# Rotary query product of a cross-attention kernel: weights stored twice side by side, nine matmuls instead of six, no doubling copy

## Chip, cores and metric

The kernel runs on one core of a Trainium2 chip. The metric is the device time of one execution in microseconds (us), the median of three runs. Engines are called PE (matmuls), DVE (vector), ACT (scalar), POOL (GpSimd) and SP (whose queue issues DMAs).

## What is computed

One block of cross-attention with multi-head latent projections, then a feed-forward block with ternary weights; batch 2, 512 query tokens of width 512, 1024 context rows of width 128, 16 heads.

```python
q_hk = (hidden_q @ Wq.T).reshape(B, S, H, K)                   # S = 512, H = 16, K = 128
q_big = _apply_rope(einsum('bshk,hkq->bshq', q_hk, w_kc_q))    # 384 wide
kv_r = _apply_rope(kv_c, sin_k, cos_k)
q_r = einsum('bshq,hqr->bhsr', q_big, W_qr)                    # R = 64: the product that is changed
k_r = einsum('bld,hdr->bhlr', kv_r, W_kr)
attn = softmax(einsum('bhsr,bhlr->bhsl', q_r, k_r))
ctx_c = einsum('bhsl,bld->bhsd', attn, kv_r)
ctx_lat = einsum('bhsd,hkd->bhsk', ctx_c, w_kc_kv)
x = x + ctx @ Wo.T
x = x + ffn(layernorm(x))      # ternary weights, activations rounded to 8 bits
```

## The kernel before

All is kept transposed, features on partitions, 512 tokens of one batch b in the free dimension. Each float32 operand of a matmul is split into a high part (rounded to float32r) and a low part (the rest), and a product is the sum of three matmuls: high by high, high by low, low by high (`three`). The work of a head is cut into groups, each of which fills one of four PSUM banks (`banks`):

- A(b): query projection, 12 matmuls; B(b, c), c = 0 to 2: its 384-wide expansion, 3 matmuls each. DVE (and for some ACT and POOL) multiplies B by cosines and sines into `rot_cos` and `rot_sin`; POOL adds them (L1055), rounds to `rot_hi` (L1061) and takes the rest `rot_lo` (L1063).
- C(b): the rotary query product with `W_qr`, 64 wide, over three chunks c. This is the group that is changed.
- K(b, half): keys; score(u), u = 0 to 7: four matmuls for 128 tokens by 1024 keys into `scores`; DVE "max" (L1323), ACT "exp" (L1185), ACT "high" (L1196) and DVE "low" (L1330) make the fp16 softmax rows; SP "turn" transposes them by DMA (L943) into `pt`.
- V(b): rows by values, 24 matmuls in 8 parts; M: the product of the two output weights; O(b, j): output, added to `acc` by DVE (L1318).

A(b), B and C of the next head are made during this one. A program for each engine runs through tables: `EVEN_PE`, `ODD_PE`, `EVEN_ACT` and so on list what the engine does in an even or odd head, in that order; `OPEN_*` is the first head with all its preparation, `LAST_*` the sixteenth. Heads 1 to 14 run as seven pairs of an odd and an even head with the same order. Engines wait on each other by semaphores: `group_full` counts groups that PE has finished, `group_hi` those whose high part ACT has taken out, `group_read` those that DVE has emptied, in DVE's order. SP loads the weights of later heads into one buffer, `load`, one lot after another (WQ, WC, WRK, WVO), each when POOL has split the one before (L386, L388).

C(b) before. The 128 columns of `wr` hold the high half of a 64-wide weight and its low half side by side. Two matmuls a chunk (`rot_hi`, then `rot_lo`, L1461) leave the high weight's product on partitions 0 to 63 and the low weight's on 64 to 127. The scores need the query on both halves, since a key tile has its high part on one half and its low part on the other. So ACT copies partitions 0 to 63 twice into `qr_hi` (L1143, L1159); DVE subtracts `qr_hi` from them into `rest` (L1270), waits for itself, and adds partitions 64 to 127 into the upper half of `qr_lo` (L1273); and ACT, some items later, copies that half to the lower one ("double", L1177). A score waits for `doubled`.

In the table of an even head ACT has "M, exp 4, high 4, C(0), exp 5, high 5, B(1, 2), double 0, V(0)"; DVE has "max 4, M, B(1, 0), B(1, 1), max 5, C(0), low 4, low 5, B(1, 2), V(0)"; PE has "score 4, M, C(0) parts 0 and 1, B(1, 0), C(0) part 2, B(1, 1), score 5, V(0)...". C(1) comes last in all three: PE begins it after O(0, 3) (even) or O(0, 0) (odd), and its part 2 is the last thing before the next head.

Of the kernel before, what the change touches and what calls it, by code (L numbers as in the profile page):

```python
# [74 lines left out]
UNGROUPED = ("score", "max", "exp", "sum", "double", "abs", "drop", "stats", "spread", "root", "deviation", "norm", "extreme", "scale", "X", "take", "first root",  # L75
# [27 lines left out]
    ("B", 0, 2, "next"), V1, ("exp", 2), ("high", 2), ("exp", 3), ("double", 1, "last"), ("high", 3), A1, ("abs", 2),  # L103
    ("M",), ("exp", 4), ("high", 4), C0, ("exp", 5), ("high", 5), ("B", 1, 2, "next"), ("double", 0, "next"), V0,
# [4 lines left out]
    ("high", 2), ("exp", 3), ("high", 3), ("double", 1, "last"), A1, ("M",), ("abs", 0), ("exp", 4), C0, ("high", 4),  # L109
    ("exp", 5), ("high", 5), ("K", 0, 0, "next"), ("K", 0, 1, "next"), ("B", 1, 2, "next"), V0, ("double", 0, "next"),  # L110
# [61 lines left out]
    ("double", 1, "last"), ("exp", 3), ("high", 3), ("exp", 4), ("high", 4), ("drop", 1), ("exp", 5), ("high", 5),  # L172
# [496 lines left out]
class SecondNorm:  # L669


    def __init__(self, nc, ctx, t):
# [115 lines left out]
def attention_heads(nc, ins, pack, sources, biases, out, t, early, raw, second):  # L788
# [3 lines left out]
    with ExitStack() as ctx:  # L792
# [339 lines left out]
        def scalar_heads(act):  # L1132
            def high_part(p, marked):
# [68 lines left out]
            def period(p):  # L1202
                for item in p.act:
# [871 lines left out]
```

## Time and profile before

| | |
|---|---|
| median of 3 runs | 858.98 us (858.0 to 860.82) |
| profiled execution, span from first to last instruction | 861.5 us |
| PE, DVE, ACT, POOL busy | 88%, 89%, 67%, 67% |
| PE clock granted | 0.97 on average, 1.00 between 84 and 667 us |
| one pair of heads | 83.3 us, seven times |
| head 0 with its preparation; last head and feed-forward | about 84 us; 194.5 us |

The profile gives the span of its execution, and no other time of it. The span is 2.5 us above the median of the runs. A busy PE is not PE at its peak: one matmul of 512 columns is shown as 0.39 us, but in a dense stretch the next begins 0.23 us later, so that their spans overlap. A DVE operation likewise overlaps the next by some 0.08 us.

### The profile page before, as it was taken

What the parts mean: (1) busy time and instruction counts of PE and PEld (TensorE: products, weight loads), DVE (VectorE), ACT (ScalarE), POOL (GpSimd) and SP (SyncE); (2) the same over time, 40 slices, a digit from 0 to 9 for tenths busy, and PEclk for the clock granted to TensorE, in tenths of its full rate; (3) what the DMA queues carried; (4) which work ended last, traced back from release to release, by engine and by line L of the source; (5) the groups of instructions that cost most, each with busy time, mean ns of one, the idle gap of its engine ahead of it and who ended that gap; (6) DMA issues with size and microseconds to landing.
All of it is one profiled execution on the core that took longest, in us unless ns stands there. A gap on an engine that the chain in (4) does not pass through costs nothing.

```text
span 861.5 us, 12578 instructions
## 1 busy us (share of the span) xinstructions
PE 757.3 (88%) x3268; PEld 487.1 (57%) x3268; DVE 766.2 (89%) x1026; ACT 573.6 (67%) x838; POOL 577.6 (67%) x581
## 2 busy tenths in 40 slices
PE   3678998989999999999999999999999675868996
PEld 3555565756666666666566656665666442424543
DVE  5799899989998999899989999999999767797895
ACT  2477677767766867687667766776777576774332
POOL 5769674867486757766776668576848474867462
PEclk9889999999999999999999999999999797889999
DMA  9216867776768576858676766677668999400000
GB/s 330 79 49 115 169 130 140 138 167 134 151 114 170 117 161 132 170 111 167 118 160 134 152 128 138 149 137 150 125 146 213 241 227 275 164 0 25 13 24 37
DMA packets 294405, 118.50 MB, mean 138 GB/s; under 512 B 271856, under 2 KB 278000, under 8 KB 294128
## 3 DMA queue, kind: packets, MB, share of 16 engines
q1 hardware_dynamic: 293568, 116.68, 62.0%
q10 hardware_dynamic: 816, 1.57, 0.5%
q8 instruction: 9, 0.15, 0.1%
q14 instruction: 12, 0.10, 0.0%
HBM read 49.02 MB, written 2.10 MB: 59 GB/s over the span
## 4 chain that ended last, share of the span: by engine, by line
PE 35%; POOL 20%; DVE 18%; issue 11%; DMA 7%; SPq 5%; ACT 3%; POOLq 1%; DVEq 0%; ACTq 0%
PE banks L1419 22%; POOL rot_cos L1055 5%; PE scores L1720 5%; DMA load<-in_pack 4%; POOL rot_lo L1063 4%; SPq L943 4%; PE scores L1507 3%; PE banks L1735 3%; DVE neg_max L1323 3%; POOL rot_hi L1061 2%; DVE rows L1330 2%; POOL rot_sin L1046 2%; DVE rot_cos L1295 2%; DVE cv_lo L1288 1%; POOL wq_lo L388 1%
## 5 line engine op out<-in xcount | busy, mean ns | idle before, releaser
L1185 ACT ACTIVATE scores<-scores,neg_max 128x1024 f32<-128x1024 f32 x128 | 139.2, 1087 | 56.1 <-DVE neg_max L1323 54.6
L1330 DVE SCALAR_TENSOR_TENSOR rows<-scores,rows 128x1024 f16<-128x1024 f32 x128 | 154.9, 1220 | 13.7 <-ACT rows L1196 12.6
L1419 PE MATMUL banks<-pt,v_hi 128*128 128x512 f16 x512 | 154.3, 383 | 12.5 <-DMA pt<-rows 11.4
L1323 DVE TENSOR_REDUCE neg_max<-scores 128x1 f32<-128x1024 f32 x128 | 155.5, 1216 | 2.9 <-PE scores L1507 2.7
L1055 POOL TENSOR_TENSOR rot_cos<-rot_cos,rot_sin 128x512 f32<-128x512 f32 x93 | 119.2, 1281 | 46.6 <-DVE rot_sin L1297 42.2
L1196 ACT ACTIVATE rows<-scores 128x1024 f16<-128x1024 f32 x128 | 130.8, 1022 | 5.2
L1063 POOL TENSOR_TENSOR rot_lo<-rot_cos,rot_hi 128x512 fp32r<-128x512 f32 x93 | 119.6, 1286 | 7.8
L1159 ACT CAST cv_hi<-banks 128x512 fp32r<-128x512 f32 x64 | 37.6, 587 | 102.6 <-PE banks L1419 101.4
L1318 DVE SCALAR_TENSOR_TENSOR acc<-banks,inv,acc 128x512 f32<-128x512 f32 x128 | 91.4, 745 | 8.0 <-PE banks L1419 4.1
L1419 PE MATMUL banks<-pt,v_lo 128*128 128x512 f16 x256 | 97.8, 382 | 0.0
L1419 PEld LDWEIGHTS banks<-pt,v_hi 128*128 128x128 f16 x512 | 44.5, 98 | 79.2 <-issue 36.4
L1946 POOL TENSOR_TENSOR hidden<-sigma,val 128x512 f32<-128x512 f32 x32 | 46.0, 1439 | 35.5 <-DVE val L1788 26.4
L1288 DVE TENSOR_TENSOR cv_lo<-banks,cv_hi 128x512 fp32r<-128x512 f32 x64 | 44.1, 689 | 26.2 <-ACT cv_hi L1159 25.1
L1061 POOL TENSOR_SCALAR rot_hi<-rot_cos 128x512 fp32r<-128x512 f32 x93 | 57.6, 619 | 14.3 <-POOL rot_cos L1055 13.3
L1720 PE MATMUL scores<-ternary,xt 128*128 128x512 bf16 x256 | 62.2, 394 | 5.3 <-DVE gate L1788 3.3
L1419 PE MATMUL banks<-m_hi,cv_hi 128*128 128x512 f32 x128 | 53.4, 417 | 14.4 <-DVE cv_lo L1288 14.4
L1419 PE MATMUL banks<-x_hi,wq_hi 128*128 128x512 f32 x128 | 53.1, 415 | 10.7 <-DVE x_lo L634 6.4
L1507 PE MATMUL scores<-kr_odd,qr_hi 128*128 128x512 f32 x128 | 57.2, 447 | 5.4 <-DVE rows L1330 5.4
L1507 PE MATMUL scores<-kr_even,qr_hi 128*128 128x512 f32 x128 | 55.0, 429 | 2.0 <-issue 2.0
L1419 PE MATMUL banks<-cv_hi,wc_hi 128*128 128x512 f32 x96 | 42.3, 441 | 12.9 <-POOL wc_lo L388 5.5
L1419 PE MATMUL banks<-x_lo,wq_hi 128*128 128x512 f32 x128 | 52.0, 406 | 0.0
L1419 PE MATMUL banks<-x_hi,wq_lo 128*128 128x512 f32 x128 | 51.9, 405 | 0.0
(211 smaller groups left out, 1824.7 us busy)
## 6 DMA issues: line engine op xcount, KB each, us to landing
load<-in_pack SPq DMA_DIRECT2D x15, 320.0 KB, 3.5
raw_chunk<-in_out_w SPq DMA_DIRECT2D x8, 512.0 KB, 5.2
raw_chunk<-in_gate_w SPq DMA_DIRECT2D x8, 512.0 KB, 4.4
raw_chunk<-in_val_w SPq DMA_DIRECT2D x8, 512.0 KB, 4.6
raw<-in_gate_w SPq DMA_DIRECT2D x8, 512.0 KB, 5.5
raw<-in_val_w SPq DMA_DIRECT2D x8, 512.0 KB, 5.2
raw<-in_out_w SPq DMA_DIRECT2D x8, 512.0 KB, 7.0
load<-in_pack SPq DMA_DIRECT2D x15, 256.0 KB, 3.3
```

Source lines behind the costliest of these rows:

```text
L1055: nc.gpsimd.tensor_tensor(total, total, rot_sin[:, c, :], ALU.add).then_inc(rot_sum, 1)
L1061: nc.gpsimd.tensor_scalar(hi, total, 1.0, 0.0, ALU.mult, ALU.add).then_inc(rot_hi, 1)
L1063: nc.gpsimd.tensor_tensor(lo, total, hi.bitcast(F32), ALU.subtract).then_inc(rot_ready, 1)
L1185: nc.scalar.activation(scores[:, u % 2, :], scores[:, u % 2, :], ACT.Exp, bias=neg_max[:, u:u + 1], accum_out=sums[:, u:u + 1]).then_inc(e ...
L1196: nc.scalar.activation(rows[:, u % ROWS, 0, :], scores[:, u % 2, :], ACT.Copy, scale=WEIGHT_LIFT).then_inc(weights_hi, 1)
L1288: return nc.vector.tensor_tensor(pair[1], src, pair[0].bitcast(F32), ALU.subtract)
L1318: return nc.vector.scalar_tensor_tensor(out=t["acc"][:, u, :], in0=src, scalar=inv[:, u:u + 1], in1=t["acc"][:, u, :], op0=ALU.mult, op1=A ...
L1323: nc.vector.tensor_reduce(neg_max[:, u:u + 1], scores[:, u % 2, :], AX, ALU.max, negate=True).then_inc(max_ready, 1)
L1330: nc.vector.scalar_tensor_tensor(out=rows[:, u % ROWS, 1, :], in0=scores[:, u % 2, :], scalar=WEIGHT_LIFT, in1=rows[:, u % ROWS, 0, :], op ...
L1419: mm = nc.tensor.matmul(out, ws[a], xs[c], start=first and n == 0, stop=last and n == 2)
L1507: mm = nc.tensor.matmul(scores[:, u % 2, half * 512:(half + 1) * 512], qr[low][:, b, j * P:(j + 1) * P], kr[odd][:, b, half * 512:(half + ...
L1720: mm = nc.tensor.matmul(ps_gv[:, n % 4, :], x, w[:, c, part_of(n // 2)], start=c == 0, stop=c == KD - 1)
```

## The change

- `wr` becomes `wr_hi` and `wr_lo`, each 128 columns: the 64 columns of a chunk twice side by side. POOL splits 128x384 elements instead of 128x192, from a source read twice.
- C takes three matmuls a chunk, nine in all instead of six, through `three` (the product of the two low parts, which the doubled arrangement had, is not made). Both halves of the partitions hold the whole query.
- ACT takes `qr_hi` out in one copy of 128x512, DVE `qr_lo` in one subtraction of 128x512. `rest`, its semaphore, the "double" items and `doubled` go; a score waits on `group_read` for C(b).
- The buffers of the second normalization's statistics move over `wv` to make room.

```diff
     def rotated(h, src):
-        split(h, 2, [t["wr"][:, :, half, :] for half in range(2)],
-              src[:, 0:CQ * R].rearrange("p (c r) -> p c r", c=CQ)).then_inc(wr_ready, 1)
+        split(h, 2, [w[:] for w in t["wr"]],
+              src[:, 0:CQ * R].rearrange("p (c o r) -> p c o r", c=CQ, o=1).broadcast_to([P, CQ, 2, R])).then_inc(wr_ready, 1)
...
                 elif kind == "C":
-                    src = banks[0:R, p.bank[marked], :]
-                    nc.scalar.copy(qr[0][0:R, group[1], :], src)
-                    out = qr[0][R:2 * R, group[1], :]
+                    out = qr[0][:, group[1], :]
...
-            def double(p, marked):
-
-                b = marked[1]
-                done = p.earlier(("C", b, "next")) if marked[-1] == "last" else p.place(("C", *marked[1:]))
-                act.wait_ge(group_read, p.read(done))
-                nc.scalar.copy(qr[1][0:R, b, :], qr[1][R:2 * R, b, :]).then_inc(doubled, 1)
-
...
-                    if kind == "C":
-
-
-                        b, low = group[1], slice(R, 2 * R)
-                        nc.vector.tensor_tensor(rest[low, b, :], banks[0:R, bank, :], qr[0][0:R, b, :].bitcast(F32),
-                                                ALU.subtract).then_inc(rest_ready, 1)
-                        dve.wait_ge(rest_ready, h.after(B, b + 1))
-                        return nc.vector.tensor_tensor(qr[1][low, b, :], banks[low, bank, :], rest[low, b, :], ALU.add)
...
                     if kind == "A":
                         pair = [x[:] for x in q]
+                    elif kind == "C":
+                        pair = [x[:, group[1], :] for x in qr]
...
-                        for half in range(2):
-                            mm = nc.tensor.matmul(out, wr[:, c].rearrange("p o r -> p (o r)"), rot[half][:, c, :],
-                                                  start=c + half == 0, stop=c + half == CQ)
+                        mm = three(out, [w[:, c].rearrange("p o r -> p (o r)") for w in wr], [x[:, c, :] for x in rot],
+                                   c == 0, c == CQ - 1)
...
                 odd = p.head.number % 2
+                places = [p.place(("C", b)) if p.first else p.earlier(("C", b, "next"))]
                 if not odd:
                     here = b or p.first
-                    pe.wait_ge(group_read, p.read(*(p.place(("K", b, half)) if here else p.earlier(("K", 0, half, "next"))
-                                                    for half in range(2))))
-                pe.wait_ge(doubled, p.head.after(B, b + 1))
+                    places += [p.place(("K", b, half)) if here else p.earlier(("K", 0, half, "next")) for half in range(2)]
+                pe.wait_ge(group_read, p.read(*places))
```

DVE in an even head, at C(0) of the next head, from max 5 to low 4 and low 5; before:

```order
L1323 TENSOR_REDUCE neg_max<-scores 128x1 [waits scores_full]
L1262 REGISTER_ALU
L1270 TENSOR_TENSOR rest<-banks,qr_hi 64x512 [waits group_hi]
L1272 REGISTER_ALU
L1273 TENSOR_TENSOR qr_lo<-banks,rest 64x512 [waits rest_ready]
L1330 SCALAR_TENSOR_TENSOR rows<-scores,rows 128x1024 [waits weights_hi] x2
```

and with the change:

```order
L1305 TENSOR_REDUCE neg_max<-scores 128x1 [waits scores_full]
L1250 REGISTER_ALU
L1270 TENSOR_TENSOR qr_lo<-banks,qr_hi 128x512 [waits group_hi]
L1312 SCALAR_TENSOR_TENSOR rows<-scores,rows 128x1024 [waits weights_hi] x2
```

Two operations with a wait between them have become one; what is before and behind them stays.

ACT at the same place, from exp 5 of the even head to V(0); before:

```order
L1143 CAST qr_hi<-banks 64x512 [waits group_full]
L1159 CAST qr_hi<-banks 64x512
L1184 REGISTER_ALU
L1185 ACTIVATE scores,sums<-scores,neg_max 128x1024 [waits max_ready]
L1196 ACTIVATE rows<-scores 128x1024 [waits row_turned1,exp_ready]
L1136 REGISTER_ALU
L1165 REGISTER_ALU [waits group_full]
L1169 COPY rot_sin<-banks 64x512 [waits rot_ready]
L1170 COPY rot_sin<-banks 64x512
L1176 REGISTER_ALU
L1177 COPY qr_lo<-qr_lo 64x512 [waits group_read]
```

and with the change:

```order
L1156 CAST qr_hi<-banks 128x512 [waits group_full]
L1174 REGISTER_ALU
L1175 ACTIVATE scores,sums<-scores,neg_max 128x1024 [waits max_ready]
L1186 ACTIVATE rows<-scores 128x1024 [waits row_turned1,exp_ready]
L1135 REGISTER_ALU
L1162 REGISTER_ALU [waits group_full]
L1166 COPY rot_sin<-banks 64x512 [waits rot_ready]
L1167 COPY rot_sin<-banks 64x512
```

The second copy of `qr_hi` and the doubling copy are gone, and exp 5 and high 5 keep their places.

## Rows read from the trace of the kernel before

**Rows 1.** The page: share of busy time, and the chain that ended last by engine.

```profile
PE 757.3 (88%) x3268; PEld 487.1 (57%) x3268; DVE 766.2 (89%) x1026; ACT 573.6 (67%) x838; POOL 577.6 (67%) x581
...
PE 35%; POOL 20%; DVE 18%; issue 11%; DMA 7%; SPq 5%; ACT 3%; POOLq 1%; DVEq 0%; ACTq 0%
```

**Rows 2.** Windows, heads 1 to 14: stretch, length, busy (instructions) by engine, PE clock.

```profile
84.00:667.00 583.00, 548.61 (x2340) 367.67 (x2339) 547.20 (x687) 419.51 (x645) 405.33 (x434) 1.00 0.71 145
```

**Rows 3.** Groups by line and form: busy us, mean ns | idle before it.

```profile
L1159 ACT CAST cv_hi<-banks 128x512 fp32r<-128x512 f32 x64 | 37.6, 587 | 102.6 <-PE banks L1419 101.4
L388 POOL TENSOR_TENSOR wr<-load,wr 128x192 fp32r<-128x192 f32 x15 | 8.9, 591 | 1.2
L386 POOL TENSOR_SCALAR wr<-load 128x192 fp32r<-128x192 f32 x15 | 5.3, 351 | 52.0 <-DMA load<-in_pack 52.0
L388 POOL TENSOR_TENSOR wc_lo<-load,wc_hi 128x384 fp32r<-128x384 f32 x15 | 16.0, 1070 | 1.2
L386 POOL TENSOR_SCALAR wc_hi<-load 128x384 fp32r<-128x384 f32 x15 | 7.7, 513 | 43.2 <-DMA load<-in_pack 43.2
```

**Rows 4.** Timeline of PE, even head: start, length, operation. C(0) part 0; B(1, 0).

```profile
490.87 0.39 PE L1461 MATMUL banks<-rot_hi,wr 128*128 128x512 f32 x1
...
491.77 0.40 PE L1419 MATMUL banks<-cv_hi,wc_hi 128*128 128x512 f32 x1
...
492.24 0.40 PE L1419 MATMUL banks<-cv_hi,wc_lo 128*128 128x512 f32 x1
```

**Rows 5.** Timeline of DVE, same place: M, B(1, 0), max 5, C(0), low 4.

```profile
491.86 0.75 DVE L1282 SCALAR_TENSOR_TENSOR m_lo<-banks,m_unit,m_hi 128x512 fp32r<-128x512 f32 x1
492.67 0.69 DVE L1295 TENSOR_TENSOR rot_cos<-banks,cos 128x512 f32<-128x512 f32 x1
...
495.08 1.22 DVE L1323 TENSOR_REDUCE neg_max<-scores 128x1 f32<-128x1024 f32 x1
496.32 0.69 DVE L1270 TENSOR_TENSOR rest<-banks,qr_hi 64x512 f32<-64x512 f32 x1
...
497.77 2.36 DVE L1330 SCALAR_TENSOR_TENSOR rows<-scores,rows 128x1024 f16<-128x1024 f32 x2
```

**Rows 6.** Timeline of POOL, then PE: from the even head to A(0) in the odd one.

```profile
495.24 1.27 POOL L1055 TENSOR_TENSOR rot_cos<-rot_cos,rot_sin 128x512 f32<-128x512 f32 x1 [0.58 <-DVE rot_sin L1297]
507.06 0.62 POOL L386 TENSOR_SCALAR wq_hi<-load 128x512 fp32r<-128x512 f32 x1 [0.21 <-DMA load<-in_pack]
506.90 0.50 PE L1461 MATMUL banks<-rot_hi,wr 128*128 128x512 f32 x1 [0.63 <-POOL rot_lo L1063]
509.11 0.50 PE L1419 MATMUL banks<-x_hi,wq_hi 128*128 128x512 f32 x1 [0.46 <-POOL wq_lo L388]
```

**Rows 7.** Timeline, second half of an odd head: ACT exp 5, high 5; DVE; POOL; PE.

```profile
453.19 1.09 ACT L1185 ACTIVATE scores<-scores,neg_max 128x1024 f32<-128x1024 f32 x1 [0.33 <-DVE neg_max L1323]
454.42 1.02 ACT L1196 ACTIVATE rows<-scores 128x1024 f16<-128x1024 f32 x1
454.63 2.36 DVE L1330 SCALAR_TENSOR_TENSOR rows<-scores,rows 128x1024 f16<-128x1024 f32 x2
460.63 1.29 POOL L1046 TENSOR_TENSOR rot_sin<-rot_sin,sin 128x512 f32<-128x512 f32 x1 [1.75 <-DVE rot_cos L1265]
465.58 0.51 PE L1461 MATMUL banks<-rot_hi,wr 128*128 128x512 f32 x1 [0.30 <-POOL rot_lo L1063]
```

**Rows 8.** Timeline: PE in head 0; DVE at the end of head 14.

```profile
57.66 0.79 PE L1419 MATMUL banks<-cv_hi,wc_hi 128*128 128x512 f32 x1 [3.05 <-DVE qr_lo L1273]
...
675.33 0.68 DVE L1270 TENSOR_TENSOR rest<-banks,qr_hi 64x512 f32<-64x512 f32 x1
676.78 1.23 DVE L1323 TENSOR_REDUCE neg_max<-scores 128x1 f32<-128x1024 f32 x1
```

**Rows 9.** Timeline of POOL, odd head: first rotation behind the key split; its wait for M.

```profile
518.77 1.29 POOL L1055 TENSOR_TENSOR rot_cos<-rot_cos,rot_sin 128x512 f32<-128x512 f32 x1
531.43 0.30 POOL L386 TENSOR_SCALAR wv_hi<-load 128x128 fp32r<-128x128 f32 x1 [0.98 <-PE banks L1419]
```

More of the change, by code:

```diff
@@ L74 @@
 A0, A1, V1, V0, C0, C1 = ("A", 0, "next"), ("A", 1, "next"), ("V", 1, "last"), ("V", 0), ("C", 0, "next"), ("C", 1, "next")
-UNGROUPED = ("score", "max", "exp", "sum", "double", "abs", "drop", "stats", "spread", "root", "deviation", "norm", "extreme", "scale", "X", "take", "first root",
+UNGROUPED = ("score", "max", "exp", "sum", "abs", "drop", "stats", "spread", "root", "deviation", "norm", "extreme", "scale", "X", "take", "first root",
              "turn", "start root", "values", "count", "variance", "inverse", "normed", "rotate", "products", "rotated",
@@ L102 @@
     ("high", 7, "last"), ("K", 1, 0), A0, ("K", 1, 1), ("exp", 0), ("high", 0), ("exp", 1), ("high", 1),
-    ("B", 0, 2, "next"), V1, ("exp", 2), ("high", 2), ("exp", 3), ("double", 1, "last"), ("high", 3), A1, ("abs", 2),
-    ("M",), ("exp", 4), ("high", 4), C0, ("exp", 5), ("high", 5), ("B", 1, 2, "next"), ("double", 0, "next"), V0,
+    ("B", 0, 2, "next"), V1, ("exp", 2), ("high", 2), ("exp", 3), ("high", 3), A1, ("abs", 2),
+    ("M",), ("exp", 4), ("high", 4), C0, ("exp", 5), ("high", 5), ("B", 1, 2, "next"), V0,
     ("exp", 6), ("high", 6), ("exp", 7), C1,
@@ L108 @@
     ("high", 7, "last"), A0, ("exp", 0), ("high", 0), ("exp", 1), ("high", 1), ("B", 0, 2, "next"), V1, ("exp", 2),
-    ("high", 2), ("exp", 3), ("high", 3), ("double", 1, "last"), A1, ("M",), ("abs", 0), ("exp", 4), C0, ("high", 4),
-    ("exp", 5), ("high", 5), ("K", 0, 0, "next"), ("K", 0, 1, "next"), ("B", 1, 2, "next"), V0, ("double", 0, "next"),
+    ("high", 2), ("exp", 3), ("high", 3), A1, ("M",), ("abs", 0), ("exp", 4), C0, ("high", 4),
+    ("exp", 5), ("high", 5), ("K", 0, 0, "next"), ("K", 0, 1, "next"), ("B", 1, 2, "next"), V0,
     ("exp", 6), ("high", 6), ("abs", 1), ("exp", 7), C1,
@@ L143 @@
     ("turn", "x", 4), ("turn", "x", 5), ("turn", "k", 1), ("abs", 2), ("rotate", 0, 0), ("rotate", 0, 1),
-    ("rotate", 0, 2), ("A", 1), ("abs", 0), ("C", 0), ("turn", "k", 0), ("double", 0), ("abs", 1), ("spread most",),
-    A0, ("K", 0, 0), ("K", 0, 1), ("Y", 3), ("values", 0), ("values", 1), ("C", 1), ("exp", 0), ("double", 1),
+    ("rotate", 0, 2), ("A", 1), ("abs", 0), ("C", 0), ("turn", "k", 0), ("abs", 1), ("spread most",),
+    A0, ("K", 0, 0), ("K", 0, 1), ("Y", 3), ("values", 0), ("values", 1), ("C", 1), ("exp", 0),
     ("high", 0), ("exp", 1), ("high", 1), ("Y", 2), ("K", 1, 1), ("M",), ("B", 0, 2, "next"), ("exp", 2), ("high", 2),
     ("K", 1, 0), ("exp", 3), ("high", 3), A1, ("exp", 4), ("high", 4), C0, ("exp", 5), ("high", 5),
-    ("B", 1, 2, "next"), ("double", 0, "next"), V0, ("exp", 6), ("high", 6), ("exp", 7), C1,
+    ("B", 1, 2, "next"), V0, ("exp", 6), ("high", 6), ("exp", 7), C1,
 )
@@ L171 @@
     ("high", 7, "last"), ("exp", 0), ("high", 0), ("exp", 1), ("high", 1), ("exp", 2), ("drop", 0), ("high", 2), V1,
-    ("double", 1, "last"), ("exp", 3), ("high", 3), ("exp", 4), ("high", 4), ("drop", 1), ("exp", 5), ("high", 5),
+    ("exp", 3), ("high", 3), ("exp", 4), ("high", 4), ("drop", 1), ("exp", 5), ("high", 5),
     ("drop", 2), ("exp", 6), ("drop", 3), ("M",), ("high", 6), V0, ("exp", 7), ("first root",), ("high", 7),
@@ L684, in __init__, with at @@
         self.links = 0
-    def at(self, rows):
+    def at(self, rows, place):
         self.rows = rows
+        self.stats = self.nc.alloc_sbuf_tensor_at("stats_second", [P, NU, 6], F32, offset=place)
+        self.mv = self.nc.alloc_sbuf_tensor_at("mv_second", [P, NU, 2], F32, offset=place + 24 * NU)
     def tile(self, u):
@@ L804, in attention_heads @@
         qr = [placed(f"qr_{x}", [P, B, S], F32R) for x in ("hi", "lo")]
-        rest = nc.alloc_sbuf_tensor_at("rest", [P, B, S], F32, offset=at["qr_lo"])
         kr = [placed(f"kr_{x}", [P, B, L], F32R) for x in ("even", "odd")]
@@ L828, in attention_heads @@
         raw.open(nc.sbuf_base, at)
-        second.at(nc.alloc_sbuf_tensor_at("normed_rows", [P, U, D], F32, offset=at["kr_even"]))
+        second.at(nc.alloc_sbuf_tensor_at("normed_rows", [P, U, D], F32, offset=at["kr_even"]), at["wv"])
         loaded, split_hi = t["loaded"], t["split_hi"]
         wq_ready, wc_ready, wr_ready, wk_ready, wv_ready, wo_ready = t["ready"]
-        rest_ready, doubled = sem("rest_ready"), sem("doubled")
         rot_sum, rot_hi, rot_ready = sem("rot_sum"), sem("rot_hi"), sem("rot_ready")
@@ L1209, in period @@
                         start.spread_most(act)
-                    elif item[0] == "double":
-                        double(p, item)
                     elif item[0] == "abs":
@@ L2008, in xattn_ffn @@
                 stack = early if side == "right" else heads
+                t["places"][name] = (nc.sbuf_base + 31) // 32 * 32
                 t[name] = [stack.enter_context(nc.sbuf_tensor(f"{name}_{half}", shape, F32R, side=side))
                            for half in ("hi", "lo")]
-            t["wr"] = early.enter_context(nc.sbuf_tensor("wr", [P, CQ, 2, R], F32R, side="right"))
+            t["wr"] = [early.enter_context(nc.sbuf_tensor(f"wr_{half}", [P, CQ, 2, R], F32R, side="right")) for half in ("hi", "lo")]
             for name in ("loaded", "split_hi", "pair_loaded", "pair_hi"):
```

1 line of the change is left out of this document (removed).

## The prediction

> **What bounds the kernel now.** I read the page first. PE is busy 88% of the span and DVE 89%, ACT and POOL 67%; the chain that ended last passes through PE for 35%, POOL 20%, DVE 18% [rows 1]. So no engine is the bound by itself: a ring of waits through several engines is. The windows say where. Heads 1 to 14 take 583 of 861.5 us, all at full PE clock, 83.3 us a pair of heads [rows 2]. The pair is therefore what has to be costed, times seven. In it I went to the timelines of the engines and noted, at each place near a C group, who waits for whom. In a dense stretch PE starts a matmul of 512 columns each 0.225 to 0.235 us: C(0) parts 0 and 1 are four matmuls between 490.87 and 491.77, and two of B(1, 0) lie between 491.77 and 492.24 [rows 4].
>
> **What the change takes away.** On DVE a C group now fills 496.32 to 497.77, 1.45 us, two operations of 0.69 and a wait [rows 5]. The subtraction that replaces them is a two-operand operation of 128x512 out of PSUM, like the four of B(1, 0) and B(1, 1), which take 492.67 to 495.08, 0.60 each with what overlaps [rows 5]. The relief is 0.84 us a group, four groups a pair: 3.4 us. On ACT two copies of 64x512 become one, which takes 0.587 as `cv_hi` does [rows 3], and the doubling copy goes. ACT relief: about 1.2 us a group, but ACT is the idlest on the ring. It counts only where DVE waits for `qr_hi`.
>
> **What it adds.** Three matmuls a C group, 0.23 each: 2.8 us a pair on PE. On POOL the split of `wr` goes from 0.351 + 0.591 to what `wc`, of the same 128x384, takes: 0.513 + 1.070, so 0.64 us a head [rows 3]. That the source is read twice has no row; the floor is no growth, the ceiling twice the old 0.94, and I take `wc`'s, since the number of elements written is the same. A score's wait on `group_read` instead of `doubled` costs nothing: C(0) is emptied by 497.77 [rows 5] and first used after 506.90 [rows 6], and C(1) is emptied before the fourth score of its head begins.
>
> **One pair, followed by its delays.** I start where part 2 of C(1) ends an odd head: PE has waited 0.30 us for `rot_lo` at 465.58 [rows 7]. Its third matmul: **+0.23**. PE is dense from there to the end of A(0). DVE waits for A(0) (its earlier relief at C(1) is spent in that wait), so all of the even head so far is late by 0.23. M, then C(0) parts 0 and 1: two more matmuls, +0.47. B(1, 0) follows them on PE, ends at 492.24 + 0.40, and DVE takes it out at 492.67, 0.03 us later, having just come to the end of M (491.86 + 0.75) [rows 4, 5]. So DVE is late by 0.70, and behind part 2 (+0.23, of which some 0.06 was DVE's own queue) by **0.87** from B(1, 1) on. The relief of C(0) on DVE comes only behind that, at 496.32. But the ring leaves DVE before it: POOL's rotation of B(1, 0) waits for `rot_sin` of B(1, 1) (idle 0.58 before 495.24) and POOL then runs without a gap to 506.8, to `wq_hi` at 507.06, before which it had 0.21 idle for a load; A(0) of the odd head waits for `wq_lo` [rows 6]. Of the 0.21 I take 0.13 as slack (my estimate; POOL needs the rest to issue): A(0) is late by **0.74**. C(1) of the even head is hidden: its parts 0 and 1 lie in PE's wait for `rot_lo` (0.63 idle before part 2, 506.90), its part 2 in the wait for `wq_lo` (0.46 idle before 509.11) [rows 6].
>
> Odd head: late by 0.74 at A(0), hence at V(1) and O, hence PE is dense to C(0). B(1, 0) is again taken out by a waiting DVE: 0.74 + 0.47; B(1, 1) and max 5: 0.74 + 0.70 - 0.06 = **1.38**. Here DVE's relief is inside the ring, because POOL next waits for DVE's B(1, 2) (idle 1.75 before 460.63) [rows 7], which stands behind C(0), low 4 and low 5. Low 4 would start 0.84 earlier than the delay says. Low 5 cannot: it needs high 5 on ACT, high 5 needs exp 5, and exp 5 waited for max 5 (0.33 idle), late by 1.38. Before, high 5 ended at 454.42 + 1.02 = 455.44 and low 5 began at 454.63 + 2.36 - 1.22 = 455.77 [rows 7], so of the 0.84 only this 0.33, less 0.04 for a semaphore, comes through: 1.38 - 0.29 = **1.09** at low 5, at B(1, 2), at POOL, and at part 2 of C(1), which waits for this POOL chain (0.30 idle before 465.58). Parts 0 and 1 are again in its wait. POOL's 0.64 for `wr` falls behind a DMA and, in the odd head, makes the first rotation (518.77, no idle before it) late by 1.3; it ends in the 0.98 that POOL waits for M before 531.43 [rows 9]. If that cover were gone, it would add up to 0.6 a pair.
>
> So a pair grows by **1.09 us**, 83.3 to 84.4, seven pairs: +7.6.
>
> **The ends.** In head 0 PE is far from dense and DVE bounds: B(0, 0) of head 1 waits 3.05 us for the bank that `qr_lo` of C(1) holds [rows 8]. Two C groups stand in DVE's dense queue before it: -1.7. C(0) of head 1, made there too, stands before a wait for transposed rows. At the end of head 14, C(1) leads straight into max 0 of the last head: ACT copies `qr_hi`, DVE works on it from 675.33, max 0 begins at 676.78 [rows 8]. One copy less (0.58) and 0.84 less on DVE, until score 0 itself is the bound: -1.1. Sum: 7.6 - 1.7 - 1.1 = +4.8. Profiled span: 861.5 to 866.3; from the median of 858.98: **863.8 us**.
>
> At the matmul price the Trainium skill differs (TensorE: Matmul & The Clock Gate, Back-to-back issue gap): it states some 131 ns per matmul of 512 columns in a sustained stream. The trace disagrees, 225 ns and more [rows 4]. By the page's figure, the seven matmuls a pair that I put on the ring would cost 0.7 us less, the pair would grow by about 0.4, and the sum would come out at no change, 859.
>
> **Rivals.**
> (A) The relief wins. DVE has the highest share [rows 1], and if the PE delay at B(1, 0) is swallowed (were DVE itself late there by as much as PE), the relief of both C(0) of a pair passes on: 7 x 2 x 0.84 = 11.8, and the ends 2.8: 844. For it: DVE ends M only 0.06 us before it takes B(1, 0) [rows 5], so it is all but late itself. Against it: all but is not enough, since the two matmuls bring 0.46. It decides if DVE comes to B(1, 0) more than 0.5 us after PE.
> The Trainium skill (Perfetto Trace Analysis, Identifying the Most-Contended Engine) tells one to relieve the engine of highest occupancy first; by that rule this is the outcome. The trace is against it so far: occupancies of 88 and 89% are alike, and the chain has twice as much of PE as of DVE.
> (B) They cancel. If the whole 0.84 in the odd head comes through (exp 5 not being what holds low 5), a pair grows by 1.38 - 0.84 = 0.54, and 3.8 - 2.8 leaves +1.0: 860. For it: ACT and DVE are only 0.3 us apart there. Against it: ACT cannot start exp 5 before max 5.
> (C) PE is the bound. All 84 added matmuls of heads 1 to 14 add up: 84 x 0.23 = 19.3, less 2.8 at the ends: +16.5, 875.5. For it: between 84 and 667 us PE is busy 548.6 of 583 [rows 2]. Against it: those spans overlap, and it waits 0.30 and 0.63 us for `rot_lo` just behind parts 0 and 1 of C(1) and 0.46 for `wq_lo` [rows 6, 7]. It decides once those waits are used up. POOL's split without its cover would be half way, 868.
>
> **How the numbers follow.** Forecast 0.52 (862 to 868), B 0.2, A 0.15, C 0.13. The range takes in B and C and leaves out A at its full price, 0.15: below, 852, half of A's gain, since how far DVE's relief gets is what I am least sure of; above, 876. A measurement of this kernel can tell some 0.3%, 2.6 us, from no change. Slower: the forecast but for its lower edge, and C, 0.58; within 0.3%: most of B and that edge, 0.2; faster: A, and what of B falls below, 0.22.
>
> **What would show it.** Right: the pair at 84.2 to 84.6 us; DVE idle about 0.7 us before B(1, 0) in both heads; low 5 of the odd head waiting for `rows` of ACT; POOL's waits at rotations of B(1, 0) and B(1, 2) as now or longer; C on PE 0.68 us a part; `qr_lo` 0.69. DVE busy some 22 us less over the span, with more idle. Wrong: a pair of 83.3 or less (A or B), with DVE going into B(1, 0) without idle; or of 86 (C), with no wait of PE left for `rot_lo`. If the wait for `wv_hi` on POOL is gone, the split was uncovered.

## The result and the profile after

| | before | with the change |
|---|---|---|
| median time | 860.09 us (856.54 to 866.47, 20 runs) | 865.25 us (860.19 to 870.69, 20 runs) |
| ratio, 95% interval | 1 | 1.0056 (1.0038 to 1.0074) |
| profiled execution, span | 861.5 us | 860.4 us |
| a pair of heads, in the trace | 83.31 us | 84.38 us |
| PE, DVE, ACT, POOL busy | 88, 89, 67, 67% | 90, 86, 62, 68% |

The change is slower by 0.56%, 5.2 us between the medians. The two profiled spans say the opposite, 861.5 and 860.4 us. They are one execution each. Their difference comes from one place: behind the M of the last head the execution of before takes 150.6 us and that of the change 143.2. Over the other twelve profiles of this study this stretch lies between 143.4 and 147.2 us, and the medians of the times don't follow it. So the spans can't be compared to a few microseconds. The heads can: in one execution the same distance comes back within 0.1 us in most pairs. The mark for a head is the start of ACT's `m_hi`, once a head. In the timeline of ACT, heads 10, 11 and 12 with the change:

```profile
495.13 0.69 ACT L1147 ACTIVATE m_hi<-banks,m_unit 128x512 fp32r<-128x512 f32 x1
...
535.79 0.69 ACT L1147 ACTIVATE m_hi<-banks,m_unit 128x512 fp32r<-128x512 f32 x1 [1.00 <-PE banks L1401]
...
579.52 0.69 ACT L1147 ACTIVATE m_hi<-banks,m_unit 128x512 fp32r<-128x512 f32 x1
```

Before, these marks are at 491.15, 531.23 and 574.48. Over the marks of heads 3 to 14 the median pair grows by 1.07, from 83.31 to 84.38. From the M of head 0 to that of head 14, seven pairs, it adds up to 7.65 us (the first pair grows by 0.63, the second by 1.64, the other five by 0.99 to 1.13). The M of head 0 comes 1.49 us earlier (64.87 to 63.38), and the last stretch, M of head 14 to M of the last, grows by 0.13. Together the last M is late by 6.3 us; the interval of the ratio holds 3.3 to 6.4.

Where a pair is cut into halves, the mark is the start of PE's last matmul of M. `m_hi` starts 0.42 or 0.43 us behind it in nearly all these heads. In the even heads of the kernel before it is 0.51, since ACT comes there from another item. That would move 0.08 us from one half to the other; the pair is the same to 0.01 by either mark. Timeline of PE and of ACT, head 10, before:

```profile
490.64 0.39 PE L1419 MATMUL banks<-wo_hi,wv_lo 128*128 128x512 f32 x1
```

```profile
491.06 0.19 ACT L1252 ACTIVATION_READ_ACCUMULATOR raw_chunk<-raw_chunk  x1
491.15 0.67 ACT L1150 ACTIVATE m_hi<-banks,m_unit 128x512 fp32r<-128x512 f32 x1
```

By PE's mark the way from the even M to the odd one was 40.14 us and is 40.65; from the odd to the even it was 43.16 and is 43.72.

The page of the change, busy time and chain, to be held beside [rows 1], and the window of heads 1 to 14 beside [rows 2]:

```profile
PE 771.4 (90%) x3364; PEld 504.5 (59%) x3364; DVE 741.3 (86%) x994; ACT 532.9 (62%) x774; POOL 588.2 (68%) x581
...
PE 31%; POOL 27%; issue 13%; DVE 12%; DMA 7%; SPq 5%; ACT 3%; POOLq 1%; DVEq 0%; ACTq 0%
```

```profile
84.00:667.00 583.00, 556.98 (x2388) 380.38 (x2387) 520.54 (x651) 379.33 (x582) 408.11 (x429) 1.00 0.70 142
```

DVE has lost 25 us of work and 6 points of the chain, and the kernel is slower. That is the lesson of the case: 25 us came off the engine with the highest share, and the time grew, because some of the added matmuls (14 us of busy time on PE) lie in front of what DVE waits for.

The groups that answer to [rows 3], by line:

```profile
L1270 DVE TENSOR_TENSOR qr_lo<-banks,qr_hi 128x512 fp32r<-128x512 f32 x32 | 21.8, 681 | 0.0
L388 POOL TENSOR_TENSOR wr_lo<-load,wr_hi 128x384 fp32r<-128x384 f32 x15 | 15.0, 1001 | 1.3
```

With its source read twice the subtraction for `wr` takes 1.00 us, about what that for `wc` takes (1.07), as the prediction had it. Now the place of [rows 4, 5] in the even head. Timeline of PE, the third matmul of C(0) part 0 and the first of B(1, 0):

```profile
495.39 0.39 PE L1401 MATMUL banks<-rot_hi,wr_lo 128*128 128x512 f32 x1
...
496.30 0.40 PE L1401 MATMUL banks<-cv_hi,wc_hi 128*128 128x512 f32 x1
```

Timeline of DVE: M, B(1, 0), max 5, C(0) in one operation, low 4, low 5:

```profile
495.91 0.74 DVE L1264 SCALAR_TENSOR_TENSOR m_lo<-banks,m_unit,m_hi 128x512 fp32r<-128x512 f32 x1
497.20 0.69 DVE L1277 TENSOR_TENSOR rot_cos<-banks,cos 128x512 f32<-128x512 f32 x1 [0.55 <-PE banks L1401]
...
499.80 1.22 DVE L1305 TENSOR_REDUCE neg_max<-scores 128x1 f32<-128x1024 f32 x1
500.93 0.68 DVE L1270 TENSOR_TENSOR qr_lo<-banks,qr_hi 128x512 fp32r<-128x512 f32 x1
501.53 1.22 DVE L1312 SCALAR_TENSOR_TENSOR rows<-scores,rows 128x1024 f16<-128x1024 f32 x1
503.34 1.22 DVE L1312 SCALAR_TENSOR_TENSOR rows<-scores,rows 128x1024 f16<-128x1024 f32 x1 [0.60 <-ACT rows L1186]
```

DVE has an idle of 0.55 before B(1, 0) that it did not have, and what it saved at C(0) ends in the 0.60 before low 5. Timeline of POOL from there, for [rows 6]:

```profile
499.96 1.27 POOL L1054 TENSOR_TENSOR rot_cos<-rot_cos,rot_sin 128x512 f32<-128x512 f32 x1 [1.22 <-DVE rot_sin L1279]
...
511.58 0.62 POOL L386 TENSOR_SCALAR wq_hi<-load 128x512 fp32r<-128x512 f32 x1
```

The rotation waits 1.22 instead of 0.58, and the 0.21 for a load that POOL had before `wq_hi` is gone.

### The profile page after: what moved, and what is told of

The parts are those of the page before. It is cut to its first block, busy times and chain, and to the rows that moved or that the text cites. A ratio compares the mean times of both kernels' runs of the same rounds, so it can differ in the third digit from the quotient of the medians.

```text
span 860.4 us, 12617 instructions
## 1 busy us (share of the span) xinstructions
PE 771.4 (90%) x3364; PEld 504.5 (59%) x3364; DVE 741.3 (86%) x994; ACT 532.9 (62%) x774; POOL 588.2 (68%) x581
## 4 chain that ended last, share of the span: by engine, by line
PE 31%; POOL 27%; issue 13%; DVE 12%; DMA 7%; SPq 5%; ACT 3%; POOLq 1%; DVEq 0%; ACTq 0%
PE banks L1401 20%; POOL rot_cos L1054 7%; PE scores L1701 4%; DMA load<-in_pack 4%; POOL rot_lo L1062 4%; SPq L942 3%; POOL rot_hi L1060 3%; PE scores L1488 3%; POOL rot_sin L1045 2%; PE banks L1716 2%; DVE neg_max L1305 2%; POOL wq_lo L388 2%; POOL wo_lo L388 2%; DVE rows L1312 1%; DMA pt<-rows 1%
```

## The experiments

All ran in five rounds beside the kernel before, and each ratio is to the runs of before on the same chip. The pair is the median over heads 3 to 14 of the profiled execution. "Even" is the distance on PE from the even M to the odd one, "odd" from the odd to the even.

| run | even | odd | pair | ratio, 95% interval |
|---|---|---|---|---|
| before | 40.14 | 43.16 | 83.31 | 1 |
| the change | 40.65 | 43.72 | 84.38 | 1.0056 (1.0038 to 1.0074) |
| six matmuls | 39.94 | 42.84 | 82.79 | 0.9936 (0.9912 to 0.9960) |
| before, nine matmuls | 41.05 | 43.98 | 85.04 | 1.0101 (1.0076 to 1.0125) |
| narrow split | 40.65 | 43.73 | 84.36 | 1.0047 (1.0025 to 1.0069) |
| six in C(1) only | 40.66 | 43.50 | 84.15 | 1.0040 (1.0012 to 1.0069) |
| DVE in pieces | 41.30 | 44.29 | 85.59 | 1.018 (1.0149 to 1.021) |
| ACT in halves | 40.69 | 43.71 | 84.43 | 1.0066 (1.0041 to 1.0090) |
| one part ahead | 40.68 | 43.47 | 84.14 | 1.0026 (1.0003 to 1.0049) |
| one part ahead, load ahead | 41.34 | 43.47 | 84.76 | 1.0079 (1.0048 to 1.0110) |
| load ahead alone | 42.06 | 43.74 | 85.78 | 1.0151 (1.0110 to 1.0192) |
| six, one part and load ahead | 41.12 | 42.69 | 83.78 | 1.0002 (0.9981 to 1.0023) |
| six, one part ahead | 39.98 | 42.66 | 82.64 | 0.9919 (0.9886 to 0.9952) |
| before, one part ahead | 39.99 | 42.95 | 82.94 | 0.9960 (0.9935 to 0.9986) |

### The two halves of the change, apart

Six matmuls: all of the change but the third matmul.

```diff
-                        mm = three(out, [w[:, c].rearrange("p o r -> p (o r)") for w in wr], [x[:, c, :] for x in rot],
-                                   c == 0, c == CQ - 1)
+                        for half in range(2):
+                            mm = nc.tensor.matmul(out, wr[0][:, c].rearrange("p o r -> p (o r)"), rot[half][:, c, :],
+                                                  start=c + half == 0, stop=c + half == CQ)
```

> The changed kernel without its third matmul a chunk (the low part of the weight times the high part of the query is left out of the product), so PE does as many matmuls as before. My theory (a ring of waits: PE's matmuls before B(1, 0) and B(1, 1) are on it, DVE's relief at C(0) comes through only in the odd head and only by 0.29 us, since exp 5 and high 5 on ACT hold low 5): a pair of heads at 83.0 us, 0.3 under the kernel before, and with 2.8 us less at the ends a ratio to before of about 0.994. Rival A (DVE is the bound, all its relief comes through): a pair at 79.9, ratio about 0.97. Rival C (PE's count of matmuls is what counts): a pair at 83.3.

Nine matmuls on the kernel before: one matmul more a chunk and nothing else.

```diff
-                        for half in range(2):
+                        for n, half in enumerate((0, 1, 0)):
                             mm = nc.tensor.matmul(out, wr[:, c].rearrange("p o r -> p (o r)"), rot[half][:, c, :],
-                                                  start=c + half == 0, stop=c + half == CQ)
+                                                  start=c + n == 0, stop=c + n == CQ + 1)
```

> The kernel before with one more matmul a chunk in C (the first of the two is issued again and added once more, so the query product differs) and all else as it was: the cost on PE alone, with no relief on DVE or ACT. My theory: the even head late by 0.74, the odd by 0.64, a pair at 84.7 us, ratio to before about 1.012. PE the bound: 12 x 0.23 = 2.8 a pair, 86.1, ratio 1.022. DVE the bound: 83.3 to 83.5, ratio 1.00.

The signs are as expected and the sizes are larger. The matmuls cost a pair 85.04 - 83.31 = 1.73 us (or, from six to nine on the changed kernel, 84.38 - 82.79 = 1.59), where the prediction had 1.38. The relief gives 0.66 us (85.04 - 84.38) or 0.52 (83.31 - 82.79), where it had 0.29. Both prices miss by about as much and in opposite directions, so the sum came out.

Where the relief comes through is seen by halves. In the odd half it is 43.98 - 43.72 = 0.26, close to the 0.29 that low 5 lets through. The rest, 41.05 - 40.65 = 0.40, is in the even half, where the prediction had none. Its place is the V(1) that PE does next, at the start of the odd head. It needs the even head's rows 7 turned by SP, the turn waits for low 7, and low 7 stands behind C(1) on DVE. Timeline of PE, last matmul of B(0, 2) and first two of V(1): before, with the change, and with nine matmuls on the kernel before:

```profile
515.70 0.40 PE L1419 MATMUL banks<-cv_hi,wc_lo 128*128 128x512 f32 x1
516.10 0.59 PE L1419 MATMUL banks<-pt,v_hi 128*128 128x512 f16 x2
```

```profile
520.41 0.40 PE L1401 MATMUL banks<-cv_hi,wc_lo 128*128 128x512 f32 x1
520.65 0.60 PE L1401 MATMUL banks<-pt,v_hi 128*128 128x512 f16 x2
```

```profile
524.25 0.39 PE L1419 MATMUL banks<-cv_hi,wc_lo 128*128 128x512 f32 x1
524.86 0.59 PE L1419 MATMUL banks<-pt,v_hi 128*128 128x512 f16 x2 [0.22 <-DMA pt<-rows]
```

A dense matmul starts 0.23 us behind the one before it. V(1) starts 0.36, 0.24 and 0.61 behind (medians of five even heads). So it waited 0.13 for its rows before, doesn't with the change, and waits 0.38 with nine matmuls and no relief, which is all but 0.02 of the 0.40. Timeline of DVE in that last run at C(1) and low 7, and of SP at the turn of rows 7:

```profile
517.68 0.68 DVE L1270 TENSOR_TENSOR rest<-banks,qr_hi 64x512 f32<-64x512 f32 x1 [0.41 <-ACT qr_hi L1159]
...
519.12 1.23 DVE L1330 SCALAR_TENSOR_TENSOR rows<-scores,rows 128x1024 f16<-128x1024 f32 x1
```

```profile
520.43 1.84 SPq L943 DMA_TRANSPOSE pt<-rows  x1
```

DVE itself waits 0.41 there for ACT's second copy of `qr_hi`. So that copy and DVE's second operation both lie on the way to low 7.

### DVE's relief, ACT's relief and POOL's split

DVE in pieces: the changed kernel, its subtraction cut into four.

```diff
+                        for rows, cols in ((slice(0, 64), slice(0, 512)), (slice(64, 128), slice(0, 320)),
+                                           (slice(64, 96), slice(320, 512))):
+                            nc.vector.tensor_tensor(pair[1][rows, cols], src[rows, cols], pair[0][rows, cols].bitcast(F32),
+                                                    ALU.subtract)
+                        src, pair = src[96:128, 320:512], [x[96:128, 320:512] for x in pair]
```

> The changed kernel with DVE's subtraction of each C group done in four pieces, (rows 0 to 63, 512 columns), (64 to 127, 320), (64 to 95, 192), (96 to 127, 192), which by 0.60 us for 512 columns should fill about 1.5 us, as the two operations and the wait did before (1.45). So DVE's relief is taken back and all else of the change left. By the steps of the prediction only 0.29 us of it comes through in a pair: 84.37 to 84.7. By the run with nine matmuls on the kernel before (85.04) the relief of DVE and ACT together is worth 0.67: if it is all DVE's, 85.0.

Timeline of DVE, C(0) in pieces and low 4, low 5; then max 0 and A(0) of the odd head:

```profile
508.77 1.45 DVE L1265 TENSOR_TENSOR qr_lo<-banks,qr_hi 64x512 fp32r<-64x512 f32 x3
510.23 0.36 DVE L1275 TENSOR_TENSOR qr_lo<-banks,qr_hi 32x192 fp32r<-32x192 f32 x1
510.63 2.36 DVE L1317 SCALAR_TENSOR_TENSOR rows<-scores,rows 128x1024 f16<-128x1024 f32 x2
...
524.50 1.22 DVE L1310 TENSOR_REDUCE neg_max<-scores 128x1 f32<-128x1024 f32 x1
525.79 0.69 DVE L1275 TENSOR_TENSOR cv_lo<-banks,cv_hi 128x512 fp32r<-128x512 f32 x1
```

The pieces take 1.86 us (508.77 to 510.63), 0.36 more than meant, so the pair is above either figure, 85.59. The run doesn't measure the relief, but it shows that DVE's part of it matters in both halves. With 1.26 us put on DVE a group, the even half grows by 0.65 and the odd one by 0.57. Low 5 has lost its wait of 0.60. A(0) of the odd head has lost the 0.78 us for which DVE waited with the change (517.35, for ACT's `cv_hi`), and is 0.59 later behind M (22.22 us with the change, 525.79 - 502.98 = 22.81 here). V(1) waits for rows 7 again (0.57 behind the matmul before it, median), and `wq_hi` waits 0.61 for its load, which stands on SP behind the turns of rows 4 and 5 and so behind low 4.

ACT in halves: two copies of 64 rows for `qr_hi`.

```diff
+                    nc.scalar.copy(qr[0][0:64, group[1], :], src[0:64, :])
+                    out, src = qr[0][64:128, group[1], :], src[64:128, :]
```

> The changed kernel with ACT's copy of each C group done in two halves of 64 rows, as before the change (0.58 us each). By the prediction ACT's relief counts only where DVE waits for qr_hi, so nothing: pair 84.3 to 84.4 us. If the difference of 0.67 us a pair between nine matmuls on the kernel before and the changed kernel is partly ACT's, 84.6 or more.

84.43: 0.05 us, next to nothing. That doesn't show that ACT has no share in the relief. Low 7 starts 0.71 us later behind M here (514.97 - 494.76 against 514.21 - 494.71), and V(1) 0.28 instead of 0.24 behind the matmul before it (head 10): the copy has just used up V(1)'s cover, and whatever DVE adds to it counts. From nine matmuls on the kernel before (41.05) to this run (40.69) the even half loses 0.36 with ACT's second copy still in place, and the copy then gives 0.04. How much of the 0.40 would be ACT's in the other order, its copy gone and DVE's two operations left, no run shows. The doubling copy of `qr_lo` was not put back in any run.

Narrow split: from the third head on, POOL splits 128x192 elements and leaves the second copy of the weights as it was, so the lower half of the product is computed with older weights.

```diff
+        wide = h.i is None and h.number < 2
+        if wide:
...
+            return
+        split(h, 2, [w[:, :, 0, :] for w in t["wr"]],
+              src[:, 0:CQ * R].rearrange("p (c r) -> p c r", c=CQ)).then_inc(wr_ready, 1)
```

> The changed kernel, but from the third head on POOL splits only the first of the two copies of the weight, 128x192 elements as before; the second copy keeps an older head's values. It takes 0.64 us a head off POOL. My theory (the split is covered by POOL's wait for M and for sines): a pair as in the changed kernel, 84.4 us. If the split stood in the open: 83.7 (odd head) or 83.1 (both).

84.36 against 84.38: the 0.64 us a head on POOL is hidden. Little of it even reaches its cover in the odd head: POOL's wait before `wv_hi` is 0.99 here and 0.85 with the whole split.

### Which matmuls count

Six in C(1) only: the first diff above, for C(1) alone.

> The changed kernel with the third matmul (low half of the weights times high half of the rotated query) left out in C(1) only; C(0) keeps nine. By the steps of the prediction C(1) costs the pair only the third matmul of part 2 in the odd head, 0.23 us, all else of it being hidden in waits for rot_lo and wq_lo: pair 84.37 less 0.23, 84.1 to 84.2 us, with PE's wait for rot_lo before part 2 of the odd head at 0.5 to 0.6 us again. If PE is the bound, all six count: 84.37 less 1.4, 83.0.

Timeline of PE, odd head, part 2 of C(1):

```profile
551.59 0.50 PE L1447 MATMUL banks<-rot_hi,wr_hi 128*128 128x512 f32 x1 [0.38 <-POOL rot_lo L1062]
```

84.15, and all of the 0.23 comes out of the odd half. So of the six third matmuls in the C(1) groups of a pair one counts, as the prediction said, and C(0) is where the price is paid. The wait for `rot_lo` comes back at 0.38, not at 0.5 to 0.6, without a bearing on the pair. With the whole change it was all but gone: the timeline of PE at the same place, one pair earlier, has

```profile
469.12 0.40 PE L1401 MATMUL banks<-m_hi,cv_lo 128*128 128x512 f32 x1
469.44 0.50 PE L1401 MATMUL banks<-rot_hi,wr_hi 128*128 128x512 f32 x1
```

which is 0.32 us from start to start, 0.09 above a dense distance. So the two third matmuls of parts 0 and 1 are hidden by a narrow margin.

### Taking C(0) out of the way

In the changed kernel part 1 of C(0) goes behind B(1, 0) and part 2 behind B(1, 1), so that DVE gets B(1, 0) three matmuls sooner. The tables of even and odd heads change alike; the lines are shortened here.

```diff
-    ("M",), part(0, 3, C0), part(1, 3, C0), ("B", 1, 0, "next"), part(2, 3, C0), ("B", 1, 1, "next"), ("score", 5),
+    ("M",), part(0, 3, C0), ("B", 1, 0, "next"), part(1, 3, C0), ("B", 1, 1, "next"), part(2, 3, C0), ("score", 5),
```

> The changed kernel with PE's order M, C(0) part 0, B(1, 0), part 1, B(1, 1), part 2, where it was M, parts 0 and 1, B(1, 0), part 2, B(1, 1): one part, 0.69 us, less before each of the two. My theory: B(1, 1) late by 0.2 instead of 0.87, a pair at 83.2 to 83.5 us, ratio to before about 0.997. If the number of matmuls, not their place, costs the time: 84.4 as in the changed kernel, ratio 1.006.

84.14, where about 83.3 was expected. The first step went as expected. Behind M, the wait of 0.55 before B(1, 0) is gone, POOL starts its rotation 0.69 us earlier (498.91 - 494.77 = 4.14 us behind M, against 499.96 - 495.13 = 4.83), and `wq_hi` is split 0.68 earlier. Then it is lost again at two waits that were not in the reckoning. Timeline of SP, POOL and PE in the even half:

```profile
511.16 1.95 SPq L940 DMA_TRANSPOSE pt<-rows  x1
513.43 0.69 SPq L905 DMA_DIRECT2D load<-in_pack  x1
```

```profile
516.56 0.51 POOL L384 TENSOR_SCALAR wc_hi<-load 128x384 fp32r<-128x384 f32 x1 [4.02 <-DMA load<-in_pack]
```

```profile
518.30 0.47 PE L1399 MATMUL banks<-cv_hi,wc_hi 128*128 128x512 f32 x1 [1.79 <-POOL wc_lo L386]
```

The load of `wc` leaves SP 18.66 us behind M, as in the changed kernel (513.82 - 495.13 = 18.69), where `wq_lo` held it too. Now `wq_lo` is early, but SP's turn of rows 6 stands ahead of the load and waits for low 6, whose scores lie behind all nine matmuls of C(0) on PE. PE then waits 1.79 instead of 0.88 for `wc_lo`. In the odd half it is score 5, which stays behind the nine matmuls whatever their order, and which max 5, exp 5 and low 5 need. Timeline of DVE, max 5 of the odd head:

```profile
540.00 1.22 DVE L1303 TENSOR_REDUCE neg_max<-scores 128x1 f32<-128x1024 f32 x1 [0.34 <-PE scores L1486]
```

The next two runs put the load of `wc` ahead of that turn on SP, in even heads.

```diff
-    ("turn", 4), ("turn", 5), ("lot", 0), ("turn", 6), ("lot", 1),
+    ("turn", 4), ("turn", 5), ("lot", 0), ("lot", 1), ("turn", 6),
```

> The order with one part of C(0) ahead of B(1, 0), and on SP, in even heads, the load of wc placed before the turn of rows 6 instead of behind it. Theory W (a second wait next in line): with one part ahead, wq_lo of the odd head was split 0.68 us earlier behind M, yet the load of wc left SP at 18.66 us behind M as before, since SP's turn of rows 6 (16.39 to 18.34) stood ahead of it, and PE then idled 1.79 instead of 0.88 us for wc_lo. So this kernel should let the load go at about 18.0 us, the odd M come 40.1 to 40.3 us behind the even M (40.83 without it), and the pair fall from 84.1 to 83.5 us (83.3 to 83.7). Theory P (PE is dense and its added matmuls are simply the bound): no change, pair 84.1.

> The changed kernel with only the SP edit (in even heads the load of wc placed before the turn of rows 6), the order of PE as in the change. Theory W: the load waits for wq_lo too, which ends 18.44 us behind M, against 18.33 for the turn; so next to nothing, pair 84.3 to 84.4 us, and only the two edits together pay. Rival: the turn alone was the wait, pair 83.7.

The first half of the expectation holds: with both edits `wc_hi` is split at 517.01 - 496.13 = 20.88 us behind M instead of 21.79, and PE waits 0.89 for `wc_lo` instead of 1.79. But the pair gets longer, 84.76 where 83.5 was expected, and with the SP edit alone 85.78 where 84.3 to 84.4 was. Timeline of SP and PE with both:

```profile
508.28 6.13 SPq L905 DMA_DIRECT2D load<-in_pack  x2
514.58 5.30 SPq L940 DMA_TRANSPOSE pt<-rows  x2
```

```profile
522.56 0.59 PE L1399 MATMUL banks<-pt,v_hi 128*128 128x512 f16 x2 [1.48 <-DMA pt<-rows]
```

A load that waits holds the whole queue: the turns of rows 6 and 7 start at 514.58, one behind the other, and V(1) waits 1.48 us for them. The expectation named what was ahead of the load and not what would stand behind it.

Then the two orders with six matmuls, and PE's order on the kernel before.

> Six matmuls in C (low half of the weights times high half of the rotated query left out), with both edits of order: one part of C(0) ahead of B(1, 0), the load of wc ahead of the turn of rows 6. With six matmuls DVE, not PE, is late at B(1, 0) (no idle before it), so the order of PE has nothing to give: pair 82.6 to 82.8 us against 82.8 with six alone. If PE's order matters here too, 82.3 or less.

> Six matmuls in C (low half of the weights times high half of the rotated query left out), with one part of C(0) ahead of B(1, 0) and SP's order as in the change. Theory: with six matmuls it is DVE that is late at B(1, 0), so PE's order gives nothing, and the loss of the kernel with both edits came from SP's order alone: pair 82.7 to 82.9 us, as with six alone (82.78). Rival: the order of PE costs something too, pair 83.2 or more.

> The kernel before with one part of C(0) ahead of B(1, 0). Theory: before the change DVE comes to B(1, 0) only 0.03 us after PE, so there is nothing to gain from PE's order: pair 83.2 to 83.3 us, ratio 1.000. The same edit under nine matmuls took the pair from 84.37 to 84.1; if it takes as much here (83.0), that gain had nothing to do with the third matmul.

With six matmuls the load ahead costs a pair 83.78 - 82.64 = 1.14 us by itself; PE's order costs nothing and gives 0.15. On the kernel before it was expected to give nothing and gives 0.37 a pair, 0.15 in the even half and 0.21 in the odd one. With nine matmuls it gave 0.24. So what this order gives does not come from the third matmuls, as the expectation's second reading says. Timeline of DVE at M, B(1, 0) and B(1, 1), as reordered:

```profile
491.76 0.75 DVE L1280 SCALAR_TENSOR_TENSOR m_lo<-banks,m_unit,m_hi 128x512 fp32r<-128x512 f32 x1
492.43 0.68 DVE L1293 TENSOR_TENSOR rot_cos<-banks,cos 128x512 f32<-128x512 f32 x1
493.03 0.68 DVE L1295 TENSOR_TENSOR rot_sin<-banks,sin 128x512 f32<-128x512 f32 x1
493.62 0.68 DVE L1293 TENSOR_TENSOR rot_cos<-banks,cos 128x512 f32<-128x512 f32 x1
```

Here B(1, 0) begins 0.67 us behind M; in [rows 5] it is 492.67 - 491.86 = 0.81. A dense DVE queue overlaps its spans by some 0.08, so a distance of 0.81 behind an operation of 0.75 is not dense: PE was already the later of the two, by 0.14, though no idle is printed. Twice 0.14 is 0.28 of the 0.37; no run places the rest.

These give two kernels that beat both. The kernel before with PE's order makes all the products of before and is at 0.9960, 858.02 us beside 862.55. Six matmuls with that order is at 0.9919, 854.72 us, but it multiplies with the high half of the rotary weights alone and is for whoever can leave the low half out.

## Why the prediction was right

It said 863.8 us, slower; the median is 865.25. Of the difference 1.11 us is the kernel before, whose median was 858.98 over three runs and is 860.09 over twenty; the growth was forecast as 4.8 us and is 5.2. The steps of the prediction, each with where it is seen:

- **Entry, +0.23 at A(0) of the even head**: `cv_lo` there was late by 0.22 (471.99 to 476.07, less the 3.86 by which the two traces stand apart at part 2 of C(1)).
- **+0.70 and +0.87 at B(1, 0) and B(1, 1)**: 0.67 (492.67 to 497.20) and 0.85 by the same count, with the idle of 0.55 for PE.
- **A(0) of the odd head 0.74 late**: 0.66 at `wq_hi`, 0.67 at `cv_lo`. POOL's whole 0.21 was slack, not 0.13 of it. That slack was a wait for the load of `wq`, which stands on SP behind the turns of rows 4 and 5, and these start when low 4 is done, right behind C(0) on DVE. With the change the load leaves SP 12.67 us behind M instead of 13.01 and is in time. With nine matmuls on the kernel before it leaves at 13.67, `wq_hi` waits 0.27 us for it (head 10), and A(0) is 0.14 later behind M than with the change (19.07 against 18.93, medians). The prediction did not ask what this load waits for.
- **Odd head, 1.38 at B(1, 1), 1.09 at low 5**: 1.35 at B(1, 1) (534.04 to 539.25, less the 3.86) and 1.07 from one even M to the next. Low 5 waits for ACT as said. In the timelines of DVE and POOL, to be held beside [rows 7]:

```profile
459.63 1.22 DVE L1312 SCALAR_TENSOR_TENSOR rows<-scores,rows 128x1024 f16<-128x1024 f32 x1 [0.60 <-ACT rows L1186]
```

```profile
464.50 1.28 POOL L1045 TENSOR_TENSOR rot_sin<-rot_sin,sin 128x512 f32<-128x512 f32 x1 [1.47 <-DVE rot_cos L1253]
```

- That POOL's wait at the rotation of B(1, 2) would be as before or longer, one of the signs named, did not come: it fell from 1.75 to 1.47. By the prediction's own steps it had to, since POOL is late by 1.38 there and DVE by 1.09.
- **Pair +1.09, seven times, 7.6**: 1.07, and 7.65 from M to M.
- **Opening -1.7**: -1.49. PE's wait in head 0 for the bank that `qr_lo` holds fell from 3.05 [rows 8] to 1.42.
- **End of head 14, -1.1**: max 0 of the last head came 0.34 earlier behind M (676.78 - 657.67 = 19.11 before, 682.60 - 663.83 = 18.77 after). The 1.1 was the gain of the last C(1); the delay by C(0) in the same head, which A(0) of the odd heads shows as 0.51 behind M, was not set against it. At the last M the term is +0.13. This one was mis-sized, by about 1.2 us. How the gain at max 0 is lost up to the last M is not traced. The medians don't show this miss either: by the marks the growth is 6.3, by the medians 5.2, and the stretch behind the last M scatters by more than the difference.
- **POOL's split hidden**: shown by the run with the narrow split. The first rotation of the odd head is late by 0.83 (518.77 to 523.46, less the 3.86), not by 1.3: 0.66 of it is A(0)'s delay.

Two prices gave the right sum from wrong parts, and that is luck. The added matmuls were put at 1.38 us a pair and cost 1.73 where nothing is taken away; the relief was put at 0.29 and gives 0.66. Both misses lie in the even half. The prediction let none of DVE's relief out in the even half: it had it spent in DVE's wait for A(0), or too late for the ring. It left out the way from C(1) over low 7 and the turn of rows 7 to V(1). By the runs the even half without the relief grows by 41.05 - 40.14 = 0.91 and with it by 0.51; the prediction has 0.74 - 0.23 = 0.51 between the two M's. The 0.51 is itself a sum that the prediction didn't have. Behind A(0), PE comes to B(0, 0) 0.65 later behind M (23.11 and 23.76, medians), where it waits for `wc_lo`, and V(1) gives back 0.13 of it, the wait for its rows that is gone. The odd half, +0.58 by the prediction's steps, is 0.56, and 0.82 without the relief, where the steps give 0.87: there price and relief are both as said.

The reading that the order of PE on the kernel before overturned is "DVE takes it out at 492.67, 0.03 us later, having just come to the end of M". DVE was the earlier one, by 0.14. For the sum this hardly matters, but it leaves less to rival A than the 0.15 it was given.

The rivals: A fell, since DVE idles 0.55 before B(1, 0) in both heads. B fell, since low 5 of the odd head waits 0.60 for ACT. C fell, since one of six third matmuls in C(1) counts. Of the two figures for a matmul the row's one held: the third matmuls of C(0) begin 0.23 us behind the second ones (495.16, 495.39).

The sum by the 131 ns of the Trainium skill (TensorE: Matmul & The Clock Gate, Back-to-back issue gap), no change, is outside the interval.

## What to carry to other kernels

Where four engines form a ring, take the late one at each meeting point, not the one with the highest share: here 25 us less on the busiest engine, with ACT's copies, bought 0.66 us a pair, and 14 us more on another, part of it in front of a take-out that already waited for it, cost 1.73. Follow every result of an engine that gets lighter or heavier to its last reader: here low 7 and its turn carried most of 0.40 us a pair, and the prediction had nothing for them. Where two engines lie on one way, putting one of them back as it was does not measure its share, since the other's relief can cover it. Read "idle" with the overlap in mind: between dense operations the distance of starts is below the printed length, and a distance above the dense one is a wait even if the view prints none. Before moving an instruction ahead in a queue, list what it will hold up if it has to wait, beside what it was held up by.

## What was not expected

- Profiles of kernels that differ only in the heads scatter by 7 us in the stretch behind the last M (143.2 to 150.6), more than the whole effect, while within one of them most pairs agree to 0.1 us. For an effect of 0.5% the pair is the instrument, and the span is not.
- DVE's pieces of 32 and 64 rows by 192 or 320 columns cost more than their columns: four pieces that hold 512 + 320 + 192 + 192 columns took 1.86 us where one of 512 takes 0.60, by which they would take 1.43.
- Two transposes one behind the other take SP's queue more than twice one: 5.30 us behind the loads ahead, where one takes 1.95. Pairs of them elsewhere in these kernels take from 4.29 us up, waits included, so what lengthens them is open.
